# Adding the FFN's bias on VectorE instead of GpSimd, with a new order of the second batch's splits

## What is computed

```python
xn = _layernorm(x, axis=-1)
s = _L0_attn_ref(xn, Wq, Wk, Wv, Wo)          # 16 heads, rotary, causal, softmax
router_logits = xf @ gate_w.T                 # xf: xn as (2048, 1024), 8 experts
routing = softmax(router_logits, axis=1)
in_scale = routing @ in_channel_scale
out_scale = routing @ out_channel_scale
ffn = xf * in_scale @ sign(weight).T * out_scale + bias
out = x + s * silu(ffn)
```

## Time and profile before

| | |
|---|---|
| median of 3 runs | 1130.0 us (1129.89 to 1130.33) |
| the profiled execution | 1129.92 us, its span 1128.1 us |
| TensorE matmul busy | 1111.2 us (98%) |
| VectorE busy | 803.0 us (71%), 1862 instructions |
| ScalarE busy | 636.2 us (56%) |
| GpSimd busy | 384.9 us (34%), 238 instructions |
| granted clock of TensorE | 1.0 throughout |

### The profile page before, as it was taken

The page is one execution under the profiler, slowest core; times in us unless marked ns, Lnnn a source line. Parts: engine busy times, 40 slices in busy tenths (PEclk is TensorE's granted clock), DMA queues, the critical chain, the costliest instruction groups (busy, mean ns, idle before and its releaser), DMA issues.

```text
span 1128.1 us, 17814 instructions
## 1 busy us (share of the span) xinstructions
PE 1111.2 (98%) x5647; PEld 927.8 (82%) x5647; DVE 803.0 (71%) x1862; ACT 636.2 (56%) x1337; POOL 384.9 (34%) x238
## 2 busy tenths in 40 slices
PE   7989999999999999999999999999999999999998
PEld 5767778888888888888888888888888887888886
DVE  7887632567677767677767677767677768899865
ACT  5744641466465665556666465666556667745341
POOL 1352665433352423424333352423424335200000
PEclk9999999999999999999999999999999999999999
DMA  9266133120211202022360211202022014687764
GB/s 368 88 246 235 57 94 125 44 66 11 65 38 45 65 9 65 9 74 65 149 223 9 65 36 47 65 9 65 9 74 65 10 65 158 201 285 229 235 208 149
DMA packets 88719, 116.40 MB, mean 103 GB/s; under 512 B 3440, under 2 KB 69104, under 8 KB 87664
## 3 DMA queue, kind: packets, MB, share of 16 engines
q1 hardware_dynamic: 88688, 116.01, 31.1%
HBM read 82.44 MB, written 33.55 MB: 103 GB/s over the span
## 4 chain that ended last, share of the span: by engine, by line
PE 90%; DVE 5%; ACT 2%; POOL 1%; issue 1%; DMA 0%; SPq 0%; DVEq 0%; ACTq 0%
PE at_proj L44 17%; PE at_proj L46 17%; PE at_proj L45 17%; PE ff_z_ps L316 7%; PE at_out L1278 7%; PE at_pt L1265 6%; PE at_score L1247 4%; PE at_score L1248 3%; PE at_score L45 1%; PE at_score L46 1%; PE at_score L44 1%; POOL ff_xs_lo L818 1%; PE at_pt L45 1%; PE at_pt L44 1%; PE at_pt L46 1%
## 5 line engine op out<-in xcount | busy, mean ns | idle before, releaser
L44 PE MATMUL at_proj<-xn_hi,w_hi 128*128 128x512 f32 x812 | 328.7, 405 | 0.0
L46 PE MATMUL at_proj<-xn_hi,w_lo 128*128 128x512 f32 x812 | 318.1, 392 | 0.0
L45 PE MATMUL at_proj<-xn_lo,w_hi 128*128 128x512 f32 x812 | 316.6, 390 | 0.0
L1971 POOL TENSOR_TENSOR at_turning<-at_turning,rope_table 128x512 f32<-128x512 f32 x64 | 83.0, 1297 | 288.0 <-DVE at_turning L1671 288.0
L46 PEld LDWEIGHTS at_proj<-xn_hi,w_lo 128*128 128x128 f32 x812 | 152.4, 188 | 33.9
L45 PEld LDWEIGHTS at_proj<-xn_lo,w_hi 128*128 128x128 f32 x812 | 153.0, 188 | 27.2
L44 PEld LDWEIGHTS at_proj<-xn_hi,w_hi 128*128 128x128 f32 x812 | 152.7, 188 | 26.6
L1469 ACT ACTIVATE at_prob<-at_score,at_neg_max 128x512 f32<-128x512 f32 (+3 forms) x256 | 133.2, 525 | 70.6 <-DVE at_neg_max L1701 70.2
L1979 POOL TENSOR_TENSOR w_lo<-w_stage,w_hi 128x1024 fp32r<-128x1024 f32 x45 | 114.5, 2559 | 162.7 <-ACT w_hi L1430 162.7
L1478 ACT ACTIVATE at_pt_hi<-at_pt 128x512 fp32r<-128x512 f32 (+1 forms) x192 | 94.0, 524 | 98.7 <-PE at_pt L1265 98.0
L1718 DVE TENSOR_TENSOR at_pt_lo<-at_pt,at_pt_hi 128x512 fp32r<-128x512 f32 (+1 forms) x192 | 111.9, 597 | 44.7 <-ACT at_pt_hi L1478 43.7
(11 more groups left out here) (233 smaller groups left out, 1960.7 us busy)
## 6 DMA issues: line engine op xcount, KB each, us to landing
w_stage<-_attn_hidden_states_dram SPq DMA_DIRECT2D x17, 512.0 KB, 6.6
z_store<-z SPq DMA_DIRECT2D x16, 512.0 KB, 2.9
w_stage<-in_L_attn_Wq_dram SPq DMA_DIRECT2D x16, 512.0 KB, 3.8
w_stage<-in_L_attn_Wk_dram SPq DMA_DIRECT2D x16, 512.0 KB, 5.1
w_stage<-in_L_attn_Wv_dram SPq DMA_DIRECT2D x16, 512.0 KB, 6.2
att_store<-at_att_t SPq DMA_DIRECT2D x32, 256.0 KB, 2.1
at_turning<-z_store SPq DMA_DIRECT2D x16, 512.0 KB, 5.7
w_stage<-in_L_attn_Wo_dram SPq DMA_DIRECT2D x12, 512.0 KB, 4.4
```

What stands on the lines that cost most here:

```text
L44: pe.matmul(out, sh, mh, start=first, stop=False, skip_group_check=reopened)
L45: pe.matmul(out, sh, ml, start=False, stop=False, skip_group_check=reopened)
L46: return pe.matmul(out, sl, mh, start=False, stop=final, skip_group_check=reopened)
```

## The change

VectorE gets `z_bias`, GpSimd loses it. In VectorE's list z_bias(0) follows z_scale(0), z_bias(1) follows first_low(3), z_bias(2) follows z_scale(2); in each later batch z_bias(n - 1), for the last tile of the batch before, follows the scaling of the eight chunks, z_bias(n) follows z_scale(n) and the norm and `x_low` behind it, and z_bias(n + 1) and z_bias(n + 2) follow their z_scale directly. In the second batch x_low(6) moves ahead of the first chunk's scaling, the statistics of tile 11 go half a tile later each, and ScalarE makes xs_high(1, 0) ahead of out_scale(3, 1). In `first_tile` the second `osc_ps` matmul moves from k = 4 to k = 6.

```diff
@@ first_tile, TensorE
-                    if k % 4 == 0 and k < KT:
-                        h = k // 4
+                    if k in (0, 6):
+                        h = min(k, 1)
@@ ScalarE
             route_copy(1)
+            xs_high(1, range(1))
             out_scale(3, 1)
-            xs_high(1, range(4))
+            xs_high(1, range(1, 4))
@@ VectorE
+            def z_bias(n):
+                dve.wait_ge(z_mul, n + 1)
+                if n == 0:
+                    dve.wait_ge(bias_in, 16)
+                dve.tensor_tensor(z[:, n % 2, :], z[:, n % 2, :], keep["bias"][:], ALU.add).then_inc(z_add, 1)
+
...
             z_scale(0)
+            z_bias(0)
             ln_stats(6, 2)
             ln_finish(6, 2)
             z_scale(1)
             first_low(2)
             first_low(3)
+            z_bias(1)
             layer_norm(8)
             x_low(4)
             x_low(5)
             router(1)
             z_scale(2)
-            ln_tile(10, 0)
+            z_bias(2)
+            x_low(6)
+            ln_tile(10, 0, (0,))
             scale(1, range(2))
-            ln_tile(10, 1, (0,))
+            ln_tile(10, 0, (1,))
             scale(1, range(2, 4))
             z_scale(3)
             for j in range(1, BATCH):
...
                 scale(j, range(4, 6))
                 if more:
-                    last = ln_tile(m + 2, 1, (1,))
+                    last = ln_tile(m + 2, 1, (0,) if j == 1 else (1,))
                 scale(j, range(6, KT))
                 if j == 1:
-                    x_low(6)
+                    last = ln_tile(m + 2, 1, (1,))
                     x_low(7)
+                z_bias(n - 1)
                 if more:
                     ln_moments(last, 2)
                     x_low(m)
@@
                 if more:
                     ln_finish(m + 2, 2)
                     x_low(m + 1)
+                z_bias(n)
                 z_scale(n + 1)
+                z_bias(n + 1)
                 if more:
                     x_low(m + 2)
                     x_low(m + 3)
@@
                 z_scale(n + 2)
+                z_bias(n + 2)
@@
                 z_scale(n + 3)
+                if not more:
+                    z_bias(n + 3)
@@ GpSimd
-            pool.wait_ge(bias_in, 16)
-            z_bias(0)
-            pool.wait_ge(first_lo, QT)
-            z_bias(1)
-            z_bias(2)
             xs_low(1, range(4))
             for j in range(1, BATCH):
                 n = QT * j
                 xs_low(j, range(4, KT))
-                z_bias(n - 1)
                 for t in range(3):
-                    z_bias(n + t)
...
                 if j + 1 < BATCH:
                     xs_low(j + 1, range(4))
-                else:
-                    z_bias(n + 3)
```

More of the change, by code:

```diff
@@ L819, in xs_low @@
                         .then_inc(xs_l[k % 2], 1)
-            def z_bias(n):
-                pool.wait_ge(z_mul, n + 1)
-                pool.tensor_tensor(z[:, n % 2, :], z[:, n % 2, :], keep["bias"][:], ALU.add).then_inc(z_add, 1)
             pool.memset(keep["ident"][:], 0.0).then_inc(idents, 1)
```

## The result

Over 21 runs each the changed kernel took 1132.05 us (1131.66 to 1133.14) and the kernel before 1130.09 us (1129.84 to 1130.76): a ratio of 1.0018, 95% interval 1.0011 to 1.0024. The change costs 2.0 us. The prediction was 1132.0.

What follows compares the result with a forecast made beforehand. TensorE, carrying 90% of the chain of waits, was taken as the bound. Gains of 0.1, 2.0 and 1.2 us against losses of 0.95, 1.25 twice, 0.86 and 0.98 summed to +2.0 us: 1132.0 us, range 1130.0 to 1133.4.

Steps and rivals of the forecast that it cites:

- term b: Start of batch 2: VectorE's added work delays scale(1, 0) by 2.1 us, in_scale(1, 4) by 0.95; +0.95 us.
- a: First tile: moving the second osc_ps matmul removes a 0.53 us wait, but ScalarE's chunk 5 split is late anyway; -0.1 us.
- c: Batch 2, x_transposes(9): TensorE's wait for x_low goes, with fewer x_low behind the scaling and no GpSimd bias; -2.0 us.
- d: Batch 2, x_transposes(10): TensorE's wait for x_low goes, as a VectorE addition is no longer held 2.40 us; -1.2 us.
- e: Last transposes of batches 2 and 3: z_bias between z_scale and x_low makes TensorE wait; +1.25 us each.
- f: Batch 3: z_bias(7) gets in before GpSimd's chunk 7 and holds it 0.98 us; +0.86 us for TensorE.
- g: Batch 4: z_bias(11) gets in before GpSimd's chunk 7, for which TensorE already waits; +0.98 us.
- Rival 1: Start of batch 2: VectorE hands on its whole lag, +2.1 us there, 1133.1 us in all; chance 0.20.
- Rival 2: Batches 3 and 4: GpSimd keeps the lock between two chunks, so no delay there; 1130.1 us, chance 0.13.
- Rival 3: All additions: 1.2 instead of 2.4 us each frees GpSimd and wins, down to 1127.4 us; chance 0.07.
- a gap in the attention: Attention, from 190 us on: no TensorE gap was expected; one would show the prediction wrong; no size given.

Runs made afterwards that it cites:

- the orders alone: Kernel before with only the second batch's new VectorE and ScalarE orders, bias still on GpSimd, first tile as before: 1129.25 us (0.9992).
- the bias alone: Kernel before with all bias additions moved to VectorE and every other order as it was: 1133.11 us (1.0027).
- The halves: Changed kernel with z_bias(7) and z_bias(11) each made as two operations of 128x512: 1130.92 us (1.0009).

## Why the prediction was right

The sum was +2.0 us and +1.96 was measured. That they agree so closely is partly luck: about 0.1 of the measured time comes from executions with a lower clock, which the sum did not have, and term b came out 0.1 smaller. The mechanism of each term can be checked by itself. Step by step, by the profiles:

- **a, the first tile (-0.1).** Right. From the stall to `x_transposes(4)` there are 41.49 - 33.89 = 7.60 us in the run that keeps the new order at full clock, 7.72 before. The changed kernel's own profile shows +1.4 in this place, by the clock alone.
- **b, the start of batch 2 (+0.95).** Right within 0.1: +0.85. Its parts, in the run with the first tile put back: `scale(1, 0)` was 67.58 - 34.21 = 33.37 us behind the stall against 31.34 before, so 2.0 late (2.1); the loop to `scale(1, 2)` 2.81 us (2.85). Only the wait inside it, at `x_transposes(7)`, was 0.26 instead of 0.55 us. In the changed kernel's profile VectorE's lag is 2.7 instead, since ScalarE's square root stood behind an output scale whose matmul ran at the lower clock, and TensorE, late itself, feels only +1.54 - 1.38 = +0.2 more.
- **c, d (-2.0, -1.2).** Right. TensorE's lead grows by 2.0 and by 1.2 at the two places once restarts are counted: TensorE's next work stands 0.79 us behind 84.31 and 90.10, and 0.92 behind 84.65 and 91.66. Counted from the first tile's stall, `x_transposes(9)` comes 0.85 us sooner than before by the orders alone and 0.26 by the bias alone, and (10) 0.86 and 1.35. So c is mostly the orders' and d the bias's.
- **e, twice (+1.25).** Right, 5.24 against 3.98 us with the addition out of the way. The expectation that each is worth 1.25 if taken back was wrong for batch 2, where VectorE is the next bound 10 us on.
- **f, g (+0.86, +0.98).** Right: chunk 7 longer by 0.97, TensorE's waits 0.59 and 1.01. The halves show that it is by turns of one instruction.

Rival 1 (the whole lag of VectorE is handed on) is out: 1.2 us of the 2.0 were given back. Rival 2 (GpSimd keeps the lock) is out by the 2.24 us. Rival 3 (halving each addition wins) is out by experiment: the bias alone costs 3.0 us. That the time stood inside what one measurement can tell, 2.26 us, was also so, by 0.3.

One reading was wrong without a consequence: the attention is not free of TensorE waits. One of 0.5 us for GpSimd, about 769 us behind its start, stands in every profile, the kernel before's too, so it cancels. And a gap in the attention was named as a sign of being wrong. The changed kernel's profile has a second one: from the attention's start to the end it takes 939.1 us, where ten others take 938.5 or 938.6. VectorE's and TensorE's rows there:

```profile
1046.82 0.69 DVE L1868 TENSOR_TENSOR w_stage<-w_stage,at_turning 128x512 f32<-128x512 f32 x1 [2.08 <-DMA w_stage<-_attn_hidden_states_dram]
```

```profile
1048.26 0.47 PE L44 MATMUL at_proj<-at_wo_sum_hi,at_a 128*128 128x512 f32 x1 [0.30 <-DVE at_partial L1855]
```

VectorE waits 2.08 us for a load from DRAM. In the kernel before it waits 0.51 us there, in the run with the first tile put back 1.58, and in neither does TensorE wait behind it; here it comes some 0.5 us later than in the latter. The run with `x_low(4)` in a wait, which keeps thirteen additions on GpSimd, shows it too (1.87 us, 938.95 to the end), and the six other runs with all additions on VectorE do not (938.5 to 938.6), so it is not the edit's. Why the load is late is open. The granted clock of 0.93 over the last ten microseconds of this profile is not the cause: two other runs had 0.91 and 0.93 there and take 938.6.

## What to carry to other kernels

Moving an operation to the faster engine is worth what its new place makes it: here four of the 16 additions (tiles 5, 9, 7 and 11, terms e, f and g) cost TensorE some 4.3 us, while the three of tiles 2, 3 and 4, with the orders, brought 3.4. VectorE's operations with two SBUF inputs and GpSimd's must be planned as one list (1.22 us became 1.95, and 1.27 became 2.24): look, for each of them, at what the other engine has been released to do at that moment, by the same semaphore above all. And a single profile can hold a fall of the clock that other executions of the same kernel do not have; find a second kernel with the same edit before explaining it.

## What the runs showed that I had not expected

The fall of TensorE's clock early in an execution: 0.57 over 34 to 38 us in the changed kernel, 0.50 over 26 to 28 us in two others, whose first tile has the old order, and 1.00 there in the other nine profiles, though three of them have the same idle stretch of 1.45 to 1.47 us in front of 34 us. In the changed kernel's profile it cost 1.4 us, where it fell on matmuls that TensorE had to do anyway. No profile ties it to the order of the first tile; the times leave room for a few tenths.

The two engines' turns go by single instructions. The Trainium skill, "SBUF — State Buffer", Who interferes with whom, says that whoever issues first holds the pair for its whole instruction. The runs agree (1.95 us for an addition of 1.22), and they show what it comes to when both engines have more to do: GpSimd's next chunk, released while VectorE's addition was under way, went second, and VectorE's next half after it.
